# A decoder of four layers on one core: a written-out place for every operation, and the third attention's normalised rows on VectorE

## The reference, cut to what matters

```python
x = x + tanh(g_xattn[0]) * attention0(layernorm(x), ctx, ctx, mask0)      # 16 heads of 64
x = x + tanh(g_ffn[0])   * ternary_gated_ffn(layernorm(x))                # inner 512
x = x + tanh(g_xattn[1]) * attention1(layernorm(x), ctx, ctx, mask1)      # 16 heads of 8
x = x + tanh(g_ffn[1])   * experts(layernorm(x))                          # top 2 of 8, capacity 269
x = x + tanh(g_xattn[2]) * attention2(layernorm(x), ctx, ctx, lens, lens) # one head of 128
x = x + tanh(g_ffn[2])   * gelu_ffn(layernorm(x))                         # inner 512, ternary
x = x + tanh(g_xattn[3]) * attention3(layernorm(x), ctx, ctx)             # 16 heads of 8, biases
x = x + tanh(g_ffn[3])   * relu2_ternary_ffn(layernorm(x))                # inner 512
```

## Time and profile before

| what | value |
|---|---|
| median of 3 runs | 484.13 us (484.13 to 485.12) |
| profiled execution, first to last instruction | 482.6 us |
| its own time | not listed beside the profile; the median lies 1.5 us above the span |
| TensorE busy (PE) | 388.5 us, 81% |
| VectorE busy (DVE) | 287.2 us, 60% |
| ScalarE busy (ACT) | 263.1 us, 55% |
| GpSimd busy (POOL) | 180.6 us, 37% |
| chain that ended last, by engine | PE 61%, ACT 11%, POOL 9%, DVE 7%, issue 7%, DMA 3% |
| mean granted clock of TensorE | 0.899 of full speed |

### The profile page before, as it was taken

The page is one execution under the profiler, slowest core; times in us unless marked ns, Lnnn a source line. Parts: engine busy times, 40 slices in busy tenths (PEclk is TensorE's granted clock), DMA queues, the critical chain, the costliest instruction groups (busy, mean ns, idle before and its releaser), DMA issues.

```text
span 482.6 us, 9945 instructions
## 1 busy us (share of the span) xinstructions
PE 388.5 (81%) x3550; PEld 281.1 (58%) x3564; DVE 287.2 (60%) x859; ACT 263.1 (55%) x781; POOL 180.6 (37%) x294
## 2 busy tenths in 40 slices
PE   3866999999997898999962999427778999889633
PEld 0645777767876665665541899315555666665522
DVE  3151575688687878665562121643546566898884
ACT  3234757676675778877631433422464766555532
POOL 3186334333424311355363000388726442221120
PEclk9597999999999999999985899855699999999955
DMA  8990000000000030000003241111000000000001
GB/s 338 394 381 6 1 2 1 1 2 2 2 1 1 1 133 1 1 13 18 20 22 93 59 130 36 45 33 27 7 0 1 3 1 1 2 2 3 3 0 43
DMA packets 7135, 22.11 MB, mean 46 GB/s; under 512 B 1215, under 2 KB 3503, under 8 KB 6575
## 3 DMA queue, kind: packets, MB, share of 16 engines
q1 hardware_dynamic: 6063, 19.38, 11.1%
q0 software_dynamic: 1024, 2.10, 1.5%
HBM read 14.60 MB, written 6.88 MB: 44 GB/s over the span
## 4 chain that ended last, share of the span: by engine, by line
PE 61%; ACT 11%; POOL 9%; DVE 7%; issue 7%; DMA 3%; SPq 0%; POOLq 0%; another core or an unknown queue 0%; DVEq 0%; ACTq 0%
PE bank L839 6%; PE bank L908 6%; PE bank L866 5%; ACT prob L565 5%; PE bank L1031 4%; PE bank L1022 3%; POOL moe_rows L488 3%; PE bank L822 3%; PE bank L854 3%; PE bank L903 3%; PE bank L917 3%; PE bank L810 3%; DVE mx L1236 3%; PE bank L888 2%; PE bank L975 2%
## 5 line engine op out<-in xcount | busy, mean ns | idle before, releaser
L565 ACT ACTIVATE prob<-bank,mx 128x128 f32<-128x128 f32 x256 | 82.3, 384 | 23.4 <-DVE mx L1236 23.2
L1236 DVE TENSOR_REDUCE mx<-bank 128x4 f32<-128x512 f32 x96 | 63.9, 682 | 41.0 <-PE bank L839 21.5
L468 POOL TENSOR_TENSOR prob<-prob,rden 128x512 f32<-128x512 f32 x32 | 33.2, 1039 | 69.2 <-DVE rden L1258 69.2
L550 ACT ACTIVATE probT<-bank 128x512 f32<-128x512 f32 x64 | 39.5, 617 | 29.9 <-PE bank L866 29.8
L866 PE MATMUL bank<-pack,prob 128*128 128x128 f32 x256 | 41.5, 286 | 7.6 <-POOL prob L468 4.6
L443 POOL TENSOR_TENSOR rstd<-rstd,minus_half 128x1 f32<-128x1 f32 x72 | 41.3, 573 | 6.0
L441 POOL TENSOR_SCALAR rstd<-mv 128x1 f32<-128x1 f32 x64 | 12.4, 193 | 83.0 <-DVE mv L1211 79.6
L866 PEld LDWEIGHTS bank<-pack,prob 128*128 128x128 f32 x256 | 28.7, 143 | 16.4 <-POOL prob L468 6.6
L488 POOL DMA_INDIRECT moe_rows<-yrows_d,row_of x16 | 16.0, 999 | 52.2 <-DMA yrows_d<-o_n 48.3
L462 POOL TENSOR_SCALAR xn<-pack,mv,rstd 128x128 f32<-128x128 f32 x32 | 25.9, 811 | 5.9 <-POOL rstd L443 5.4
L565 ACT ACTIVATION_READ_ACCUMULATOR prob<-bank,mx 128x1 f32 x128 | 27.9, 218 | 0.0
(11 more groups left out here) (233 smaller groups left out, 965.2 us busy)
## 6 DMA issues: line engine op xcount, KB each, us to landing
yrows_d<-moe_rows SPq DMA_DIRECT2D x2, 1510.0 KB, 21.2
pack<-pack_d SPq DMA_DIRECT2D x1, 2112.0 KB, 15.7
expert<-experts_d SPq DMA_DIRECT2D x4, 514.0 KB, 8.5
pack<-experts_d SPq DMA_DIRECT2D x4, 514.0 KB, 5.1
pack<-pack_d SPq DMA_DIRECT2D x1, 2048.0 KB, 10.3
xrows_d<-moe_rows SPq DMA_DIRECT2D x1, 1080.0 KB, 21.0
moe_rows<-xrows_d SPq DMA_DIRECT2D x8, 135.0 KB, 3.0
yrows_d<-o_n SPq DMA_DIRECT2D x8, 135.0 KB, 1.8
```

What stands on the lines that cost most here:

```text
L468: pool.tensor_tensor(part, part, r.to_broadcast([P, GH, P]), ALU.mult).then_inc(E[A0]["norm"].sem, 1)
L550: act.activation(dst, src, ACT.Identity if kw else ACT.Copy, **kw).then_inc(E[layer][name].sem, 1)
L565: act.activation(prob[:, g % 2, P * j:P * j + P], bank[S_BANK[g % 2]][:, P * j:P * j + P], ACT.Exp, bias=mx[:, g % 2, j:j + 1], **kw).then ...
L1236: dve.tensor_reduce(out, bank[S_BANK[g % 2]][:, :].rearrange("p (h t) -> p h t", h=GH), AX.X, ALU.max, negate=True).then_inc(E[layer]["max ...
```

## The change

`PLAN`, the lags, the slots and the hooks go. `walk` now takes every operation of every batch at a place of its own, a number in a table; an operation that is a generator goes back into the queue 0.203 further on at each of its yields. So the order may differ from batch to batch.

```diff
-def walk(eng, plan, stages, before={}, after={}, run=lambda layer, fn, it, *args: fn(it, *args)):
...
+def walk(stages, once=(), run=lambda layer, fn, it, *args: fn(it, *args)):
+    queue = []
+    for layer, entries in stages.items():
+        for b in range(B):
+            for fn, *args, places in entries:
+                if places[b] is not None:
+                    queue.append((places[b], len(queue), run, (layer, fn, Item(b, b), *args)))
+    for at, fn in once:
+        queue.append((at, len(queue), fn, ()))
+    while queue:
+        at, n, begin, args = head = min(queue, key=lambda entry: entry[0:2])
+        queue.remove(head)
+        rest = begin(*args)
+        if rest is not None:
+            if next(rest, stages) is not stages:
+                queue.append((at + TURN, n, lambda rest=rest: rest, ()))
...
@@ GpSimd: the third attention's rs ends after the inverse root; two lines of its table
-                if layer in (F0, F3):
+                if layer in (F0, F3, A2):
                     return
...
-                    [(3, rs, A2), (2, fetch_ahead)],
+                    (fetch_ahead, (320.9, 329.516, 330.548, 282.7, 307.074, 344.178, 316.285, 335.572)),
+                    (rs, A2, (303.889, 312.924, 332.356, 335.48, 340.482, 342.485, 352.272, 355.962))],
...
@@ VectorE: the new operation
+            def centre2(it):
+                wait(dve, A2, "rs", it)
+                wait(dve, A2, "xt", it.back(2))
+                dve.tensor_scalar(xn2[:, it.k, :], x_sb[:, it.b, :], mv[A2][:, it.k, 0:1], rstd[A2][:, it.k, 0:1], ALU.subtract, ALU.mult
+                                  ).then_inc(E[A2]["xn"].sem, 1)
...
-                    [[(3, norm2), (0, sum_stats)]],
+                    (sum_stats, (313.79, 314.935, 316.602, 317.835, 326.075, 328.018, 337.917, 341.97)),
+                    (centre2, (315.49, 317.935, 319.202, 320.135, 331.375, 331.718, 340.717, 345.67)),
...
@@ TensorE: the transpose waits for VectorE's event; a hook has become a wait in its operation
-                    wait(pe, layer, "rs", it)
+                    wait(pe, layer, "xn" if layer == A2 else "rs", it)
...
+                if it.rep == 0 and layer == F0:
+                    pe.wait_ge(tern_dve, 9)
...
-                    [(2, probsT, A0, 2), (0, proj0, "k", 0), (1, scores0, 0)],
+                    (scores0, 1, (30.459, 44.956, 64.949, 82.901, 94.596, 115.583, 129.371, 141.644)),
...
```

More of the change, by code:

```diff
@@ L74, in at @@
         return self.per * item.b + (self.base + (self.per if j is None else j))
-def steps_of(offsets):
-    last = max(at + B + LAG[n] for n, at in offsets.items())
-    return [("steps", [(n, t - at) for n, at in offsets.items() if 0 <= t - at < B + LAG[n]]) for t in range(last)]
-def turns(*parts):
-    parts = list(parts)
-    while parts:
-        for p in list(parts):
-            if next(p, parts) is parts:
-                parts.remove(p)
-            else:
-                yield
-def walk(eng, plan, stages, before={}, after={}, run=lambda layer, fn, it, *args: fn(it, *args)):
-    def stage(layer, s, loop, lag, fn, *args):
-        rep = s - lag
-        if 0 <= rep < B:
-            held = run(layer, fn, Item(rep if loop is None else 2 * loop + rep, rep), *args)
-            if held is None:
-                yield
-            else:
-                yield from held
-    def slot(layer, s, entries, loop=None):
-        for entry in entries:
-            if entry is None:
-                yield
-                continue
-            for_turns = entry if isinstance(entry, list) else [entry]
-            yield from turns(*[stage(layer, s, loop, *e) for e in for_turns])
-    def single(layer, s, loop=None):
-        for n in range(SLOTS):
-            for _ in slot(layer, s, stages[layer][n], loop):
-                pass
-    for what in plan:
-        if what[0] == "steps":
-            for at in what[1]:
-                before.get(at, lambda: None)()
-            for n in range(SLOTS):
-                for _ in turns(*[slot(layer, s, stages[layer][n]) for layer, s in what[1] if layer in stages]):
-                    pass
-            for at in what[1]:
-                after.get(at, lambda: None)()
-        elif what[1] in stages:
-            _, layer, first, passes = what
-            if eng is None:
-                for s in range(first, first + 2 * passes):
-                    single(layer, s)
-            else:
-                with eng.Fori(0, passes) as i:
-                    for s in range(first, first + 2):
-                        single(layer, s, i)
@@ L147 @@
 A0, F0, A1, ROUTE, MOE, A2, F2, A3, F3 = range(9)
-LAG = [3, 2, 5, 2, 2, 4, 7, 5, 5]
 KIND = ["first", "gated", "second", "route", "moe", "first", "inner", "second", "gated"]
 SIDE = [0, 1, 0, 1, None, 0, 1, 0, 1]
-PLAN = (steps_of({F0: 4, A0: 0, A1: 6, ROUTE: 11})
-        + [("steps", [(MOE, s)]) for s in range(NE + 2)]
-        + steps_of({A2: 0, F2: 3, A3: 8, F3: 13}))
+TURN = 0.203
 def build(nc, packs, mask0_d, mask1_d, lens_d, experts_d, xrows_d, yrows_d, out_d):
@@ L533, in _ @@
                 A3: [
-                    [],
-                    [],
-                    [],
-                    [None, (4, rs, A3)]],
+                    (rs, A3, (368.359, 378.814, 383.414, 396.498, 402.631, 406.21, 434.623, 447.743))],
                 F3: [
-                    [(4, rs, F3)],
-                    [],
-                    [(5, rms_hid)],
-                    []],
-            }
-            walk(pool, PLAN, stages, before={(A2, 0): first_fetches}, after={(A0, 1): masks})
+                    (rs, F3, (404.691, 412.897, 431.423, 449.944, 457.927, 465.518, 468.277, 488.33)),
@@ L547, in _ @@
+                    (rms_hid, (432.377, 441.168, 457.54, 461.669, 469.444, 481.373, 511.844, 511.878))]}
+            walk(stages, [(7.6, masks), (277.7, first_fetches)])
         @block.scalar
@@ L742, in _ @@
             prepare()
-            walk(act, PLAN, stages, before={(MOE, 0): route_exp, (A2, 0): lambda: k4_sb(1, 0)})
+            walk(stages, [(264, route_exp), (310.9, lambda: k4_sb(1, 0))])
         @block.tensor
@@ L1208, in ln_stats @@
                     wait(dve, BEFORE[layer], "resid", it)
+                wait(dve, layer, "rs", it.back(2))
                 do = chain(layer, "ln", it)
@@ L1370, in hid2_stats @@
                 wait(dve, F2, "gelu", it)
+                wait(dve, F2, "rs_hid", it.back(2))
                 do = chain(F2, "hid", it)
@@ L1594, in _ @@
             prepare()
-            walk(dve, PLAN, stages, before={(A0, 3): means, (MOE, 0): weigh_experts, (A2, 0): start_last, (F3, 0): squared_bias})
+            walk(stages, [(65.3, means), (266.8, weigh_experts), (310, start_last), (295, squared_bias)])
 def pack(arrays, pack_):
```

371 lines of the change are left out of this document (209 added, 162 removed).

## The result

The changed kernel takes **506.39 us** (median of 4 runs, 505.49 to 507.20); the kernel before, beside it, 484.13 (483.57 to 485.12). The ratio is 1.0458, with an interval of 1.0435 to 1.0481: **slower by 22 us**. The forecast was 467.3 with a range up to 481.0, so the sign was wrong and the range missed. The profiled execution spans 505.4 us where before's spanned 482.6: 22.8 us to account for.

A forecast was written before the change was run, and what follows sets the result against it. TensorE was taken to bound 48 to 240 us, GpSimd A2's start, VectorE and TensorE nearly full from 408 to 456. Gains 4.4 + 4.6 + 1.9 + 4.5 + 1.4 = 16.8 off 484.13 gave 467.3 us, range 453 to 481.

The forecast's parts named there:

- What bounds the kernel: TensorE sets 48 to 240 us, with 12.8 us idle to find; GpSimd paces A2's start; VectorE and TensorE nearly full later.
- The start: Earlier statistics and values bring batch 1's masks and the first product of probabilities forward: 4.4 us gained.
- A0, F0 and A1: Other products fill TensorE's recurring waits in A0 and at the hand-over: 4.6 us gained.
- keys behind exponentials: In A0's batches 5 and 6, ScalarE's copy of keys stands behind two groups of exponentials: 2.1 us charged.
- those 2.2 us go: At the hand-over, TensorE's waits of 0.71 and 1.50 us ahead of A0's last masks vanish.
- The new list puts other products into both gaps: A0's steady part: TensorE's waits for ScalarE's copies of keys, 2.3 us, and of the transpose, 2.2, get filled.
- The end of the routing: VectorE's division follows A1's last product at once, on the path to the last scatter and experts: 1.9 us gained.
- A2 and F2: GpSimd loses 7.7 us as rows move to VectorE, while batch 2's fetch comes later: 4.5 us gained.
- the forecast 6.0 later: In A2, batch 0's maximum, queued on VectorE behind batch 2's later fetch, sum and statistics, comes 6.0 us later.
- F2, A3 and F3: More products stand between TensorE's three waits for ScalarE's copy ahead of F2's output: 1.4 of 3.7 us gained.
- Queues block in the dense stretch: Rival: unready operations block lists; TensorE loses 1.4 us in each of A0's and A1's sixteen batch steps: 494.3 us, chance .13.
- The announced sign of failure: TensorE's busy share from 48 to 240 us falling under 93% would show the forecast wrong.

The follow-up runs named there:

- e6: e1 with the first values ahead of the queries on TensorE and batch 1's statistics between the two copies of values on VectorE: 478.81 us, ratio 0.9871.
- e1: The changed kernel with A0, F0, A1 and ROUTE back in the old order in steps on all four engines: 480.37 us, 0.9903 of the kernel before.
- e9 to e12: e1 with the change's order in A0 to ROUTE up to 66, 100, 165 us, or only after 152 us: 481.38, 484.51, 490.21, 499.81 us.
- e5: The changed kernel with five blocked copies or exponentials of A0 and F0 moved ahead in ScalarE's and VectorE's lists: 505.07 us, 1.0419 of the kernel before.
- e7: e1 with A1's last output and division ahead of batch 5's choice: 481.58 us, 0.9934 of the kernel before.
- e3: The kernel before, all in steps, with only A2's normalised rows moved from GpSimd to VectorE: 479.31 us, ratio 0.9889.
- e14: The changed kernel with both halves of A1's scores 1.5 later in TensorE's list, all eight batches: 537.10 us, 1.1071 of the kernel before.

## Why the prediction was wrong

**What bounds the kernel: right, and the reason it failed.** TensorE's 12.8 idle us from 48 to 240 are all that a better order could find there. What the sum left to one rival is that a worse order can lose much more: it lost 23.7.

**The start (4.4): about half right at its place, little of it on the path.** The first normalised probabilities came 3.6 us sooner, near the forecast 34 us. But the first transposes of them gained only 1.7 (37.76 against 39.49): TensorE's products of batch 1 (L847), for which it waits 1.66 us, now stand ahead of them. By itself the start brings batch 0's output 2.8 us forward and the first fetch 0.7 (e6), and the end by 1.6, which is within the noise.

**A0, F0 and A1 (4.6): the step that failed.** The prediction looked at the waits that the new order would remove and charged one place, keys behind exponentials, with 2.1 us. The trace has 28.8 us lost there. Even the hand-over, "those 2.2 us go", kept two waits, 0.71 and 1.17. The reading error is the sentence "The new list puts other products into both gaps": that an operation stands in a gap says nothing unless it is ready when the gap comes, on a list in which it may itself be waited for. e1 shows that the front's lists are the cause, e9 to e12 that they cost along their whole length, e5 that the five clearest places don't hold it. How the 28.8 us fall on the four lists stays open.

**The end of the routing (1.9): right at its place, wrong on the path.** The division follows the product at once (274.28 behind 274.21), and lateness falls from 27.1 to 25.4 by the first fetch. But there the product was so late that VectorE, done with the choice, waited 3.27 us for it. Applied alone the move brings the division 1.7 us forward and gains nothing: GpSimd's scatters are the path to the experts (e7). The prediction had put the division there.

**A2 and F2 (4.5): nearly right.** Batch 0's maximum starts 16.9 us after the first fetch, where it was 10.9 (318.79 in the earlier trace rows, minus 307.87): the forecast 6.0 later. The first gelu follows 35.0 us after the first fetch instead of 38.7: 3.7 sooner, where "some 5" was said. F2's transpose is only 0.9 sooner, not 4: it now stands in TensorE's list behind other batches' work. `centre2` (by-source row: min, median and max ns):

```profile
L1243 DVE TENSOR_SCALAR pack<-pack,mv,rstd x8: 315/346/431, 341.6 to 370.7; 128x128 f32<-128x128 f32 x8
```

0.35 us, none near 1.1. In steps the move alone gains as much (e3: some 4 of its 5.2), with the first F2 transpose at 336.05 us, 29.3 behind its first fetch where it was 33.6 behind the earlier trace rows. So the gain needs no new fetch order.

**F2, A3 and F3 (1.4): not seen.** Between the first gelu and the end lateness grows from 21.8 to 22.8: 1.0 us lost in this profile. Others with the same places there need up to 1.8 us less from the first fetch to the end (170.3 against 172.1), so the sign is not sure.

**The rivals.** "Queues block in the dense stretch" was what happened, at a chance of .13: it priced each of 16 batch steps at 1.4 us and decided from 0.8; measured are 28.8 / 16 = 1.8. Its time, 494.3, was 12 us low, since it paired 22.4 lost with 12.2 gained, where 28.8 were lost and some 6 gained. The argument against it, "TensorE has other work in most of the new gaps", is the same error as above. That the average came so near is in part luck: the loss was not one group of exponentials in each step but many different waits. The announced sign of failure, a TensorE share under 93% from 48 to 240, came: 159.07 of 192 is 83%.

## What to carry to other kernels

An engine's list is right only together with the lists of the others: before changing a list where the bounding engine is busy nine tenths of the time, ask for each new neighbour whether it is ready when its turn comes, and price what stands behind it if it is not. When every place in an order changes at once, do not credit the waits that vanish without charging for the new neighbours, and test the order of one stage at a time with the old one in the others. Separate a change of order from a change of engine: here the second was worth some 4 us by itself and could hardly be seen beside the first.

## What was unexpected

**The size of small shifts.** Putting sixteen groups of scores 1.5 later on one engine cost 30.7 us (e14 against the change), of which TensorE's lower clock is about a third.

**VectorE beside GpSimd.** The forecast feared slow `centre2` beside the fetches, after the 1.07 us row. The one at 351.70 us took 0.34 and began inside a fetch's span on GpSimd:

```profile
351.45 0.95 POOL L438 DMA_INDIRECT moe_rows<-yrows_d,row_of  x1 [0.30 <-issue]
351.70 0.34 DVE L1243 TENSOR_SCALAR pack<-pack,mv,rstd 128x128 f32<-128x128 f32 x1
```

The Trainium skill (SBUF — State Buffer, Who interferes with whom) says that a VectorE tensor_scalar in a two-port mode and a GpSimd instruction exclude each other; as the forecast had applied it, to a fetch, no row here shows it: the longest `centre2` took 0.43 us, and the fetches have a mean of 0.97 us where they had 1.00. Whether `centre2` ran in such a mode no run here tells.
